# First tile of a gated attention and experts kernel begun on half of its context: another order of loads and of GpSimd, ScalarE and TensorE work

## What is computed

```python
# xattn: a causal long convolution (kernel of length L = 1024 per head) of products of the context with itself
kv  = einsum("bhil,bhjl->bijhl", ctx, ctx)          # 8 x 8 products per head, symmetric in i and j
y   = irfft(rfft(kv, 2L) * rfft(ssm_kernel, 2L))[..., :L] + kv * D
out = einsum("bijhl,bhil->bjhl", y, layernorm(x))
x   = x + tanh(g_xattn) * out
# ffn: layernorm, softmax gate, top 2 of 8 experts, gated products with a low-rank part
x   = x + tanh(g_ffn) * experts(layernorm(x))
```

## Times and profile before

| | us |
|---|---|
| median of 3 runs | 1497.64 |
| lowest, highest | 1496.67, 1497.68 |
| the profiled execution | 1494.09 |
| its span, first to last instruction | 1492.3 |
| TensorE busy | 1432.7 (96%) |
| VectorE busy | 1152.5 (77%) |
| GpSimd busy | 1117.9 (75%) |
| ScalarE busy | 775.3 (52%) |

### The profile page before, as it was taken

One profiled execution on the slowest core, in us unless ns is written; L12 is line 12 of the kernel. 1 busy time (PEld: TensorE's weight loads), 2 busy tenths in 40 slices (PEclk: granted clock), 3 DMA queues, 4 the chain that ended last, 5 costly groups with the idle time before them and its releaser, 6 DMA issues. The chain is left out here.

```text
span 1492.3 us, 34506 instructions
## 1 busy us (share of the span) xinstructions
PE 1432.7 (96%) x10676; PEld 1383.5 (93%) x10677; DVE 1152.5 (77%) x1922; ACT 775.3 (52%) x1359; POOL 1117.9 (75%) x985
## 2 busy tenths in 40 slices
PE   3999999999999999999999999989899999999994
PEld 3999999999999999999999999989899999999994
DVE  3999999999999999999999999968444454444442
ACT  5656665666566656675666566510333433443341
POOL 6998999899989998999899989615355555555552
PEclk9999999999999999999999999999999999999997
DMA  6666776777676767676767676536589999999984
GB/s 203 202 223 214 225 217 220 218 220 218 218 223 215 218 219 224 213 212 225 216 222 215 222 212 226 178 131 169 135 193 250 259 249 234 251 270 223 228 176 72
DMA packets 114345, 315.49 MB, mean 211 GB/s; under 512 B 25152, under 2 KB 25664, under 8 KB 114304
## 3 DMA queue, kind: packets, MB, share of 16 engines
q1 hardware_dynamic: 93728, 239.96, 51.8%
q0 software_dynamic: 20576, 75.04, 22.6%
HBM read 215.66 MB, written 100.86 MB: 212 GB/s over the span
## 5 line engine op out<-in xcount | busy, mean ns | idle before, releaser
L542 DVE TENSOR_REDUCE oT<-z 128x128 f32<-128x1280 f32 x256 | 380.5, 1486 | 8.9
L643 PE MATMUL Y<-kvhi,t_hi 128*128 128x288 f32 x1280 | 382.8, 299 | 0.0
L644 PE MATMUL Y<-kvlo,t_hi 128*128 128x288 f32 x1280 | 377.9, 295 | 0.0
L645 PE MATMUL Y<-kvhi,t_lo 128*128 128x288 f32 x1280 | 377.3, 295 | 0.0
L315 POOL TENSOR_TENSOR kvlo<-kv,kvhi 128x1152 fp32r<-128x1152 f32 x128 | 341.0, 2689 | 0.0
L298 POOL TENSOR_TENSOR kv<-cT 128x768 f32<-128x768 f32 x128 | 238.5, 1864 | 8.6 <-DMA cT<-in_c 8.6
L643 PEld LDWEIGHTS Y<-kvhi,t_hi 128*128 128x128 f32 x1280 | 240.9, 188 | 0.6
L644 PEld LDWEIGHTS Y<-kvlo,t_hi 128*128 128x128 f32 x1280 | 241.1, 188 | 0.0
L645 PEld LDWEIGHTS Y<-kvhi,t_lo 128*128 128x128 f32 x1280 | 241.0, 188 | 0.0
L525 DVE TENSOR_TENSOR z<-Y,qT 128x512 f32<-128x512 f32 x256 | 176.9, 691 | 28.9 <-PE Y L645 17.0
L1264 PE MATMUL GU<-wt_hi,xu_hi 128*128 x568 | 170.4, 300 | 0.0
(11 more groups left out here) (178 smaller groups left out, 3339.1 us busy)
## 6 DMA issues: line engine op xcount, KB each, us to landing
cT<-in_c SPq DMA_DIRECT2D x32, 768.0 KB, 8.1
t_hi<-khi SPq DMA_DIRECT2D x64, 384.0 KB, 3.8
t_lo<-klo SPq DMA_DIRECT2D x64, 384.0 KB, 5.1
u_hi<-kshi SPq DMA_DIRECT2D x64, 320.0 KB, 5.9
u_lo<-kslo SPq DMA_DIRECT2D x64, 320.0 KB, 6.9
x_nat<-in_x SPq DMA_DIRECT2D x32, 512.0 KB, 4.2
out<-x_new SPq DMA_DIRECT2D x32, 512.0 KB, 4.9
normed<-n SPq DMA_DIRECT2D x32, 512.0 KB, 7.6
```

The costliest lines, as they stand in the source:

```text
L542: nc.vector.tensor_reduce(oT[p][:, 2 * r:2 * r + 2, h * IB:(h + 1) * IB], view(z[s][:], [[ZC, 2], [2, IB], [2 * IB, ZS], [1, 2]]), AX.XY, ...
L643: nc.tensor.matmul(out, w_hi[:, w], m_hi[:, c, :], start=start, stop=False)
L644: nc.tensor.matmul(out, w_hi[:, w], m_lo[:, c, :], start=False, stop=False)
L645: return nc.tensor.matmul(out, w_lo[:, w], m_hi[:, c, :], start=False, stop=stop)
```

## The change

Half of the context is loaded by itself ahead of x; each of the four kernel rows has a semaphore of its own, and each of the first windows is fetched when its row is out; the other half of the context, the second set of windows, `ag` and the first weights follow. GpSimd does the work on chunks 0 to 3 with the difference ahead of chunks 4 to 7. ScalarE begins with a square root of a constant, does the squares and the first half ahead of the layernorm of x, and `ag` last. TensorE begins with 20 matmuls that nobody reads, then conv(0, 0, 0), the transposes and shared(0, 0). The low part of `ag` moves behind the first tile on VectorE.

```diff
@@ SP
                 eng.dma_start(dcol[:], dskip_d).then_inc(k_in, 16)
+                eng.dma_start(cT[0][:, 0], c_d[0][:, 0]).then_inc(c_first, 16)
                 eng.dma_start(x_nat[0][:], x_d[0]).then_inc(x_in[0], 16)
-                eng.dma_start(cT[0][:], c_d[0]).then_inc(c_in[0], 16)
                 for s, d in constants.first:
                     eng.dma_start(s[:], d).then_inc(const_in, 16)
-                eng.dma_start(ag[:], ag_d).then_inc(const_in, 16)
-                eng.dma_start(w_raw[:], w_d[0]).then_inc(w_in, 16)
                 eng.wait_ge(khi_done, 1)
-                eng.dma_start(khi_d, krow_hi.bitcast(F32)).then_inc(k_out, 16)
+                eng.dma_start(khi_d, krow_hi.bitcast(F32)).then_inc(k_out[0], 16)
...
-                eng.wait_ge(k_out, 64)
...
-                for h in range(HT):
-                    windows(h, h)
+                eng.wait_ge(k_out[0], 16)
+                window_hi(0, 0)
+                eng.wait_ge(k_out[1], 16)
+                window_lo(0, 0)
+                eng.wait_ge(k_out[2], 16)
+                sum_window_hi(0, 0)
+                eng.wait_ge(k_out[3], 16)
+                sum_window_lo(0, 0)
+                eng.dma_start(cT[0][:, 1], c_d[0][:, 1]).then_inc(c_in[0], 16)
+                windows(1, 1)
+                eng.dma_start(ag[:], ag_d).then_inc(ag_in, 16)
+                eng.dma_start(w_raw[:], w_d[0]).then_inc(w_in, 16)
                 eng.dma_start(cT[1][:], c_d[1]).then_inc(c_in[1], 16)
@@ GpSimd
-                head(0, 0, 0, 16)
+                products(0, 0, 0, 0, None)
+                difference(0)
+                low_half(0, 0, 0)
+                low_difference(0, 0)
+                products(0, 0, 1, 0, None)
+                low_half(0, 0, 1)
@@ ScalarE
+                eng.wait_ge(eps_ready, 1)
+                nc.scalar.activation(sd[:], epsc[:], ACT.Sqrt).then_inc(root_ready, 1)
                 eng.wait_ge(k_sum, 1)
                 nc.scalar.copy(krow_hi, krow).then_inc(khi_done, 1)
                 eng.wait_ge(ks_sum, 1)
                 nc.scalar.copy(ksum_hi, ksum).then_inc(kshi_done, 1)
-                eng.wait_ge(const_in, 48)
+                squares(0, 0, 0)
+                high_kv(0, 0, 0)
+                sum_x(0, 0, 16)
+                high_difference(0, 0)
+                eng.wait_ge(root_ready, 1)
+                square_x(0, 0)
+                normalize(0, 0)
+                high_kv(0, 0, 1)
+                eng.wait_ge(const_in, 32)
                 nc.scalar.activation(gt[:], gate[:], ACT.Tanh).then_inc(gate_ready, 1)
+                take_q(0, 0)
+                eng.wait_ge(ag_in, 16)
                 nc.scalar.copy(ag_parts[:, :, 0, :], ag[:]).then_inc(ag_split, 1)
-                root(0, 0, 16)
-                normalize(0, 0)
-                head(0, 0, 0)
-                take_q(0, 0)
@@ TensorE
-                eng.wait_ge(const_in, 48)
-                transpose_x(0)
+                eng.wait_ge(eps_ready, 1)
+                keep_busy(nc, Y[1][:, 0, 0:2 * P], gated[:, 0:P], gated[:], 20)
+                eng.wait_ge(const_in, 32)
...
+                    if first:
+                        eng.wait_ge(t_in[0], 64)
+                        conv(0, 0, 0)
+                        transpose_x(0)
+                        shared(0, 0)
+                    else:
+                        shared(i, 0)
+                        conv(i, 0, 0)
```

More of the change, by code:

```diff
@@ L159, in attend @@
         ks_sum, kshi_done, kslo_done = sem("ks_sum"), sem("kshi_done"), sem("kslo_done")
-        k_out = sem("k_out")
+        k_out = [sem(f"k_out{n}") for n in range(4)]
+        eps_ready = sem("eps_ready")
+        c_first, ag_in, root_ready = sem("c_first"), sem("ag_in"), sem("root_ready")
         ag_split = sem("ag_split")
@@ L228, in windows @@
[L228 to L232, removed]
-                for h in range(HT):
-                    windows(h, h)
+                eng.wait_ge(khi_done, 1)
@@ new lines, in window_lo, with sum_window_hi, sum_window_lo, windows @@
+                def window_lo(n, h):
+                    eng.dma_start(t_lo[h][:].bitcast(F32), kernel_window(klo_d, n, KW, TW)).then_inc(t_in[h], 16)
+                def sum_window_hi(n, h):
+                    eng.dma_start(u_hi[h][:].bitcast(F32), kernel_window(kshi_d, n, KS, SW)).then_inc(t_in[h], 16)
+                def sum_window_lo(n, h):
+                    eng.dma_start(u_lo[h][:].bitcast(F32), kernel_window(kslo_d, n, KS, SW)).then_inc(t_in[h], 16)
+                def windows(n, h):
+                    window_hi(n, h)
+                    window_lo(n, h)
+                    sum_window_hi(n, h)
+                    sum_window_lo(n, h)
@@ L288, in products @@
                     n = 2 * i + h
-                    eng.wait_ge(c_in[p], have)
+                    if have is None:
+                        eng.wait_ge(c_first, 16)
+                    else:
+                        eng.wait_ge(c_in[p], have)
                     if not (isinstance(n, int) and n < 1):
@@ L306, in difference, with low_half @@
                     eng.wait_ge(square_done, 2 * n + 1)
-                    if not (isinstance(n, int) and n < 1):
+                    if isinstance(n, int) and n < 1:
+                        eng.wait_ge(kv_done, 1)
+                    else:
                         eng.wait_ge(diffhi_done, n)
                     nc.gpsimd.tensor_tensor(diff[:], kv[:, 0:2, :], kv[:, 2:4, :], ALU.subtract).then_inc(diff_done, 1)
-                def low_kv(n, h):
[L312 to L317, removed]
+                def low_half(n, h, half):
+                    eng.wait_ge(kvhi_done, 2 * n + half + 1)
+                    c0 = half * (NC // 2)
+                    nc.gpsimd.tensor_tensor(kvlo[h][:, c0:c0 + NC // 2, :], kv[:, c0:c0 + NC // 2, :],
+                                            kvhi[h][:, c0:c0 + NC // 2, :].bitcast(F32),
+                                            ALU.subtract).then_inc(kvlo_done[h], 1)
+                def low_kv(n, h):
+                    low_half(n, h, 0)
+                    low_half(n, h, 1)
                 def low_difference(n, h):
@@ L332, in head @@
                     if isinstance(i, int) and i == 0 and h == 1:
-                        eng.wait_ge(k_out, 64)
+                        for done in k_out:
+                            eng.wait_ge(done, 16)
                     low_kv(2 * i + h, h)
                     low_difference(2 * i + h, h)
-                head(0, 0, 0, 16)
+                products(0, 0, 0, 0, None)
[4 more added lines that the diff above has]
+                low_half(0, 0, 1)
                 def body(i, p, k, last=False):
@@ L355, in squares @@
                 def squares(n, p, h):
-                    eng.wait_ge(kv_done, 2 * n + 1)
+                    if isinstance(n, int) and n < 1:
+                        eng.wait_ge(c_first, 16)
+                    else:
+                        eng.wait_ge(kv_done, 2 * n + 1)
                     for half in range(2):
@@ L389, in take_common, with sum_x @@
                     nc.scalar.copy(common[h][:], shared_y).then_inc(common_done, 1)
-                def root(i, p, have):
+                def sum_x(i, p, have):
                     eng.wait_ge(x_in[p], have)
@@ L396, in root, with square_x @@
                     nc.scalar.activation(xn[:], x_nat[p][:], ACT.Identity, accum_out=sum1[:]).then_inc(sd_done, 1)
+                def root(i, p, have):
+                    sum_x(i, p, have)
+                    square_x(i, p)
+                def square_x(i, p):
                     eng.wait_ge(sd_done, 5 * i + 1)
@@ L728, in turn @@
                     mm.then_inc(turned, 1)
-                eng.wait_ge(const_in, 48)
-                transpose_x(0)
+                eng.wait_ge(eps_ready, 1)
+                keep_busy(nc, Y[1][:, 0, 0:2 * P], gated[:, 0:P], gated[:], 20)
+                eng.wait_ge(const_in, 32)
                 def body(i, p, first=False, last=False):
-                    shared(i, 0)
-                    conv(i, 0, 0)
+                    if first:
[3 more added lines that the diff above has]
+                        shared(0, 0)
+                    else:
+                        shared(i, 0)
+                        conv(i, 0, 0)
                     if not first:
@@ L755, in _ @@
                 body(0, 0, first=True)
+                body(1, 1)
                 eng.wait_ge(ag_split, 2)
-                body(1, 1)
                 with eng.Fori(1, NT // 2 - 1) as k:
```

23 lines of the change are left out of this document (12 added, 11 removed).

## The result

| | kernel before | changed kernel |
|---|---|---|
| median, us | 1497.66 (6 runs) | 1506.43 (6 runs) |
| lowest, highest | 1494.82, 1500.07 | 1503.66, 1507.2 |
| profiled execution, span | 1494.09, 1492.3 | 1506.63, 1504.8 |
| ratio, 95% interval | | 1.0053 [1.0042, 1.0065] |

The changed kernel is slower, by 0.53%, about 8 us by the ratio (the medians differ by 8.8); forecast was a gain of 4.2 us. In what follows the low clock level of TensorE is 1.2 GHz and the high one 2.4 GHz.

A forecast was written before the change was run, and what follows sets the result against it. TensorE bounds the first block's long middle, GpSimd its start. D, the latest of GpSimd's path 23.8, `ag` 25.9 and clock 23.8 or 26.7, was taken as 26.2: 2.4 + 1.8 = 4.2 us gain, 1493.4 us, range 1490.4 to 1496.8.

The forecast's parts named there:

- gain formula: Second tile's shared matmuls: gain is 28.62 - D plus GpSimd's 1.8 us lead; forecast 4.2 us.
- moves by 6: VectorE's start: x is turned and taken at about 25 us, not 31, so VectorE moves by 6.
- rival on the side of slower: TensorE's start: the warm-up runs past T, ending at 40 us; loss 16.0 us, 1513.6 us, chance 0.07.
- D: Start of GpSimd's second difference (L309), at 28.62 us in the kernel before; forecast 26.2 us.
- long middle: First block, 60 to 960 us: TensorE's, busy 894 of 900 us; it brings its end forward as much as its start.
- T: When the last of TensorE's four first windows lands: between 15.7 and 19.7 us, taken as 17.4.
- the windows come late: Rival: fetching by piece gains nothing; T 19.7, low clock, D 29.0, gain 1.4 us, 1496.2 us, chance 0.25.
- The clock: TensorE from T to the shared result: 5.3 us at the high level, 8.2 at the low; leaned to low, not firmly.
- The warm-up: TensorE's 20 float32 matmuls at the start: from about 1.2 us, ending at 13.4, about 4 us idle before T.
- the upper bound: Cost of one float32 warm-up matmul as four split products: 0.88 us at the low level, 0.50 at the high.
- `ag`: ScalarE's wait for it before take_common: landing at 24.7 us in queue order, which puts D at 25.9.
- GpSimd's own path: GpSimd from its first products at 5.8 us to the two products of half tile 1: D at 23.8 at the best.

The follow-up runs named there:

- e1: Changed kernel with the low part of `ag` taken on GpSimd, behind the first w_lo, instead of VectorE: 1494.23 us, ratio 0.9987 to the kernel before.
- e3: Changed kernel with the `ag` subtraction replaced, at its place, by a tensor_reduce reading one SBUF operand: 1496.19 us, one execution.
- g2: Changed kernel with GpSimd waiting for VectorE's `ag` subtraction before the second products of half tile 3: 1495.40 us, one execution.
- f4: e1 with SP waiting for the first four windows before issuing the other half context and second window set: 1495.04 us, one execution.
- f3: f1 and f2 together, with the DMA of `ag` behind the first constants: 1493.96 us, one execution.
- f1: e1 with GpSimd's first products waiting for VectorE's last subtraction of the kernel rows: 1494.59 us, one execution.
- f2: e1 with 34 warm-up matmuls in place of 20: 1494.99 us, ratio 0.9987 to the kernel before.
- g1: e1 with 37 warm-up matmuls and `ag` loaded with the constants, GpSimd not held back: 1494.17 us, ratio 0.9979 to the kernel before.
- e2: Kernel before with only the low part of `ag` moved behind the first tile on VectorE, TensorE's wait moved too: 1504.69 us, ratio 1.0036.

## Why the prediction was wrong

**The step that failed is one that is not in it.** The change moves the low part of `ag` behind the first tile on VectorE; the front lists it, and the prediction costs every other moved piece of `ag` (its DMA, ScalarE's copy) but not this one. It is a term put at nothing: the gain formula was to hold "as long as TensorE and VectorE move by more", and VectorE was then checked by its start alone ("moves by 6"), without the new work behind the first tile. By its length, 0.22 us, that work was worth no line; it took 10.11 us, and with the low clock behind it cost TensorE 10.9 us. Its cost is that of the place: it is VectorE's only operation in that stretch with two SBUF operands (the multiplies and joins read Y from PSUM, the matmul results' memory, `x_new` reads OP from there, the sums have one operand), and it left an idle stretch of GpSimd for one where GpSimd is at work without a gap, as the earlier trace rows said (35.5 of 35.7 us). e1, e3 and g2 show it, each in its own way. The rival on the side of slower had the wrong mechanism: the warm-up ended at 11.7.

**The formula held at the second tile, and failed for the time.** The prediction called it wrong if these matmuls move by another amount than the span does, and so it was: 1.5 us earlier, and a span 12.5 us longer. It says when the second tile starts, and nothing of what VectorE does in it. Gain = 28.62 - D + 1.8 met the second tile's shared matmuls within 0.1 us in five of six kernels of the table; in f4, where D was later than before, it was 0.5 us off, as TensorE's own path then counts. The gain lasts: f3's 3.7 us at the second tile are 3.7 us at half tile 5 (93.07 against 96.79). So the reasoning that the long middle hands on what the start gives was right, and so is its other side: it handed on a lateness of 9.4 us too.

**D was too early: 28.85, not 26.2.** Its terms:
- *T*: 20.16, not 17.4, and outside the ends of 15.7 and 19.7. The last row was issued at 10.15, not at 8.72, but landed in 2.6 us, at 12.75, within the forecast 12.2 to 13.1, and its window was issued at 12.81. The window's transfer was mis-sized: 7.3 us, where the ends had 3.5 and 6.6. In f1 the last row's issue moved by 0.9 us and T did not. The rival "the windows come late" had the time right (19.7, D 29.0); why they are slow is open.
- *The clock*: low, as I leaned to. From T to the end of shared it was 27.48 + 0.30 - 20.16 = 7.6 us, for 8.2 in the sum.
- *The warm-up*: 10.47 us for 20, against 12.2 estimated; at the high level 0.43 each against 0.50 (in f2, 43 records from 8 to 17 us, two to a matmul). The choice of the upper bound was right. It ended 1.7 us sooner and T came 2.8 later than forecast, so TensorE was idle for 8.45 us and not 4.
- *`ag`*: landed at 26.1, not 24.7, just behind the last window ahead of it (25.5), as forecast by the order of the queue. But ScalarE was busy with the turned x until 27.6 and did not wait for it. With the clock high it might have mattered; f3 loads it early, and no run has the one without the other.
- *GpSimd's own path*: ready at 26.4, not 23.8. It started 0.8 us later than thought and lost another 1.6 us to the collision of its products with VectorE's subtractions of the kernel rows, a second term put at nothing, though both stood in the trace of the kernel before (VectorE at 6.2 to 8.4 us): an earlier start of one engine laid its work over the two-operand work of the other.

Without the subtraction the changed kernel would have been the rival of the late windows: 1.6 us by the formula, forecast at 1.4; e1, which is that, measured 0.9987, about 1.9 us. So the forecast of 4.2 us would have missed even then: D and the subtraction are two separate failures.

## What to carry to other kernels

Before an instruction is moved, look at what the engine it shares something with does at the new place: a VectorE operation with two SBUF operands of 0.2 us can cost 10 us where GpSimd works without a gap. It cost 0.32 us on GpSimd itself, and 0.21 us with one SBUF operand or with GpSimd held back for 0.4 us. When an early start is bought for one engine, price by the engine that has the least lead behind it; the gain is that lead plus what its last dependent step moves by, and it can be read from two rows. The warm-ups of TensorE that kept the high level here ended 1.54 us or less before the work began; D came 1.1 us (e1 to g1) earlier by it, together with the early `ag`.

## What the runs showed that was not expected

- A two-operand subtraction of VectorE that began while a GpSimd instruction ran waited for that one to end (1.34, 1.31, 2.65, 2.65 and 2.56 us in place of 0.2 or 0.94), but once, in the changed kernel, through five ends of instructions to the sixth, 10.11 us. The Trainium skill ("SBUF — State Buffer", Summary: rules for kernel authors) says that of the two who comes second blocks until the first is done; the five short ones agree with that, the 10.11 us go beyond one instruction. It works the other way round too: in the changed kernel VectorE's subtraction of 6.29 was first and kept its 1.35 us, and the GpSimd product that began at 6.60 took 2.72 for 1.80. What decides whether VectorE is let in at the end of one is open; all six executions of the changed kernel lay at 1503.66 or above, and e2's fell in two groups.
- With 2.55 us of idleness in front of it TensorE's level still fell, after the work had begun again; in the earlier trace rows 2.77 us of idleness did no harm, and 1.54 us did none in f3.
- The windows' transfers took 9.4 us from the first issue to the last landing (10.66 to 20.1) where they took 7.9 before (13.18 to 21.1): the last of the four was issued 2.15 us behind the first, for 1.34 before. Issuing the first 2.5 us earlier gained 1.0.
